# Layer 1 on four split filter steps, tree additions by accumulating transfers, and field copies on GpSimd, in a two-layer interaction kernel

## The reference

```python
z = einsum('bhd,bmd->bhmd', x0, prev)        # products of fields with the layer before
cur = relu(einsum('bpd,pn->bnd', z, W[0]))   # 128 outputs
prev = cur
```

## Time and profile before

| | us |
|---|---|
| median of 3 runs (lowest, highest) | 946.62 (946.28, 947.04) |
| the profiled execution, its own time | 947.22 |
| its span, first to last instruction | 945.3 |
| PE busy | 881.0 |
| DVE busy | 765.0 |
| ACT busy | 691.3 |
| POOL busy | 773.2 |

### The profile page before, as it was taken

How to read it: one execution, slowest core, us unless ns; L and a number is a source line. 1 busy time by engine, 2 the same in 40 slices (tenths; PEclk the granted TensorE clock), 3 DMA queues, 4 the chain that set the end, 5 groups by cost and what they waited for, 6 DMA issues and landing times.

```text
span 945.3 us, 17955 instructions
## 1 busy us (share of the span) xinstructions
PE 881.0 (93%) x3551; PEld 650.2 (69%) x3551; DVE 765.0 (81%) x2391; ACT 691.3 (73%) x2347; POOL 773.2 (82%) x582
## 2 busy tenths in 40 slices
PE   0289999999999999999999999999999999999989
PEld 0157777777777777777777777777777777777753
DVE  4068888889888888898888889988888899888893
ACT  2058777787878777878787778787877777877762
POOL 7768899888888999988889989887777877777772
PEclk9999999999999999999999999999999999999999
DMA  6031222222112222221122222211222222102000
GB/s 175 13 105 51 75 75 75 73 72 71 32 50 70 73 74 73 74 71 34 46 69 74 73 74 74 74 38 37 67 71 71 71 71 71 47 29 66 1 1 0
DMA packets 41436, 58.13 MB, mean 61 GB/s; under 512 B 7265, under 2 KB 16033, under 8 KB 41410
## 3 DMA queue, kind: packets, MB, share of 16 engines
q1 hardware_dynamic: 37314, 55.76, 18.6%
q0 software_dynamic: 4096, 2.11, 1.4%
HBM read 54.79 MB, written 3.05 MB: 61 GB/s over the span
## 4 chain that ended last, share of the span: by engine, by line
PE 53%; DVE 26%; issue 14%; POOL 4%; DVEq 2%; DMA 0%; ACT 0%
PE bank L836 38%; DVE acc L721 18%; PE bank L774 12%; POOL rows L331 4%; DVE pair L587 4%; DVE cur_low L598 2%; DVE parts L721 1%; DVEq L718 1%; PE bank L879 1%; DVEq L240 0%; PE bank L866 0%; PE bank L867 0%; DVE sum L629 0%; PE bank L874 0%; DVEq L707 0%
## 5 line engine op out<-in xcount | busy, mean ns | idle before, releaser
L521 ACT ACTIVATE parts<-bank,x 128x128 f32<-128x128 f32 x2048 | 584.8, 385 | 143.5 <-PE bank L836 140.1
L721 DVE SCALAR_TENSOR_TENSOR acc<-bank,x,acc 128x128 f32<-128x128 f32 x1792 | 485.6, 343 | 97.2 <-PE bank L836 96.0
L836 PE MATMUL bank<-w_high,cur_high 128*128 128x512 f32 x1024 | 440.5, 430 | 10.9 <-DVE acc L721 10.0
L836 PE MATMUL bank<-w_low,cur_high 128*128 128x512 f32 x1024 | 401.4, 392 | 0.0
L836 PE MATMUL bank<-w_high,cur_low 128*128 128x512 f32 x992 | 389.1, 392 | 0.0
L352 POOL TENSOR_TENSOR half<-parts 128x1024 f32<-128x1024 f32 x127 | 307.1, 2418 | 92.4 <-DVE parts L721 91.9
L836 PEld LDWEIGHTS bank<-w_high,cur_high 128*128 128x128 f32 x1024 | 192.5, 188 | 105.9 <-DVE acc L721 29.3
L836 PEld LDWEIGHTS bank<-w_low,cur_high 128*128 128x128 f32 x1024 | 193.0, 188 | 48.8 <-issue 14.8
L836 PEld LDWEIGHTS bank<-w_high,cur_low 128*128 128x128 f32 x992 | 186.4, 188 | 41.8
L352 POOL TENSOR_TENSOR half<-half 128x512 f32<-128x512 f32 x127 | 165.5, 1303 | 10.0
L378 POOL DMA_INDIRECT rows_next<-table_dram,ids_next x96 | 92.5, 963 | 17.5 <-issue 7.0
(11 more groups left out here) (77 smaller groups left out, 485.8 us busy)
## 6 DMA issues: line engine op xcount, KB each, us to landing
shifts<-x_scratch SPq DMA_DIRECT2D x155, 256.0 KB
x<-x_scratch SPq DMA_DIRECT2D x31, 256.0 KB, 2.9
x_scratch<-turned SPq DMA_DIRECT2D x31, 64.0 KB, 1.5
rows_next<-table_dram,ids_next POOLq DMA_INDIRECT x96
wt<-w_top_dram SPq DMA_DIRECT2D x2, 512.0 KB, 8.9
x_scratch<-turned SPq DMA_DIRECT2D x31, 32.0 KB, 1.8
rows<-table_dram,ids_sb POOLq DMA_INDIRECT x32, 2.4
w_sb<-w_ab_dram SPq DMA_DIRECT2D x1, 256.0 KB
```

The costliest lines, as they stand in the source:

```text
L521: ins = nc.scalar.activation(parts[q][ab][:, at:at + N2], act_bank[ab][:, i * N2:(i + 1) * N2], ACT.Copy, scale=x0[u][:, h, 2 * q + ab:2 * ...
L721: nc.vector.scalar_tensor_tensor(out=dst, in0=dve_bank[e % 2 * 2 + ab][:, i * N2:(i + 1) * N2], scalar=x0[u][:, h, 2 * q + ab:2 * q + ab + ...
L836: return nc.tensor.matmul(dst[:], cur_half[u][:, cols], w1_half[:, fields], **flags)
```

## The change

Layer 1's steps 1 to 4 are all split; the slots of the side work are new. The tree's first addition is made by an accumulating transfer that POOL issues for each tile. There is one `left`; POOL adds its halves too (`sum_left`), ACT rectifies the total (slot 20) and DVE adds it (slot 24). The copies for x0 and `turn_in` are POOL's.

```diff
-TREE = 3
-LEFTS = 2
+TREE = 2
+LAST_TREE = 3
-SPLIT = (1, 2)
+SPLIT = (1, 2, 3, 4)
-ACT_PAIR_HIGH = {5: 1, 13: 2}
-ACT_HIGH16, DVE_LOW16 = 9, 12
-PE_PRODUCT = {17: 1, 19: 3, 21: 0, 23: 4, 24: 2}
+ACT_PAIR_HIGH = {5: 1, 8: 2, 9: 3, 16: 4}
+ACT_HIGH16, DVE_LOW16 = 12, 16
+PE_PRODUCT = {18: 1, 19: 2, 21: 3, 22: 0, 24: 4}
-ACT_X0 = 21
-ACT_TURN, PE_TURN, ACT_TURNED = 1, 6, 8
-ACT_LEFT, DVE_TOTAL, DVE_FOLD = 20, 24, 28
+PE_TURN, ACT_TURNED = 3, 4
+ACT_TOTAL, DVE_FOLD = 20, 24
...
+            def add_halves(pair_no, q, whole):
+                pool.wait_ge(act_prod, (pair_no + 1) * (2 * EACH))
+                pool.wait_ge(mac, (pair_no + 1) * (2 * MACS))
+                nc.gpsimd.tensor_tensor(mark[:], mark[:], mark[:], ALU.subtract)
+                width = EACH * HG * N2 // 2
+                for ab in range(2 if whole else 1):
+                    nc.gpsimd.dma_start(parts[q][ab][:, 0:width], parts[q][ab][:, width:2 * width],
+                                        accum_op=ALU.add).then_inc(added[ab], 16)
             def sum_parts(chunk, pair_no, t):
...
+                pool.wait_ge(added[t % 2], (pair_no + 1) * 16)
+                src = parts[t // 2 % 2][t % 2]
+                nc.gpsimd.tensor_tensor(half[t % 2][:], src[:, 0:512], src[:, 512:1024], ALU.add).then_inc(tree, 1)
+                pool.wait_ge(tree, tile * TREE + 1)
+                nc.gpsimd.tensor_tensor(left[:, t % DC, :, :].rearrange("p l n -> p (l n)"),
+                                        half[t % 2][:, 0:256], half[t % 2][:, 256:512], ALU.add).then_inc(tree, 1)
+            def sum_left(chunk):
+                pool.wait_ge(tree, (chunk + 1) * (DC * TREE))
+                pool.wait_ge(total_rectified, chunk + 1)
+                nc.gpsimd.tensor_tensor(total.rearrange("p (t n) -> p t n", t=DC), left[:, :, 0, :], left[:, :, 1, :],
+                                        ALU.add).then_inc(totalled, 1)
...
             def block_body(k, next_block, one_after):
+                for t in range(0, tiles, 2):
+                    whole = next_block or t < tiles - 2
                     if t % DC == 0 and (next_block or t < tiles - DC):
+                        pair_lows(k * CPB + t // DC + 1, (2, 3))
+                    add_halves(k * (tiles // 2) + t // 2, t // 2 % 2, whole)
+                    for s in (t, t + 1):
+                        if (next_block and s < rows_at) or (one_after and s > rows_at):
+                            for f in late[s]:
+                                gather(f)
+                    if t % DC == 0:
+                        if next_block or t < tiles - DC:
+                            copy_x0(k, t // DC + 1)
+                        if next_block or t // DC + 3 < CPB:
+                            copy_turn_in(k, t // DC + 3)
+                    if t % DC == 2 and (next_block or t < tiles - DC - 2):
+                        pair_lows(k * CPB + t // DC + 2, (0, 1))
+                    for s in (t, t + 1) if whole else (t,):
+                        sum_parts(k * CPB + t // DC, k * (tiles // 2) + t // 2, s)
+                        if s % DC == DC - 1:
+                            sum_left(k * CPB + t // DC)
...
-        def act_left(act, c, u, pairs_before):
+        def act_total(act, c, pairs_before):
+            act.wait_ge(totalled, c + 1)
             act.wait_ge(paired, pairs_before)
+            nc.scalar.activation(x4_bank[:], total, ACT.Relu).then_inc(total_rectified, 1)
...
         def dve_fold(dve, c, k):
+            dve.wait_ge(total_rectified, c + 2)
+            nc.vector.tensor_tensor(block_sum(k), x4_bank[:], block_sum(k), ALU.add).then_inc(folded, 1)
...
             if step == order[0]:
-                wait(pe, summed, c)
-                if turn:
-                    pe.wait_ge(turned_ready, c + 1)
-                if pair16_bank(c) is cur_bank:
-                    pe.wait_ge(low16, c + 1)
+                pe.wait_ge(low16, c + 1)
```

More of the change, by code:

```diff
@@ L94, in dlrm_tower @@
         shifts = [sb(f"shifts_{i}", [P, STEPS, COLS]) for i in range(2)]
-        pair = [sb(f"pair_{i}", [P, COLS]) for i in range(STEPS - 1)]
+        pair_low = [sb(f"pair_low_{i}", [P, COLS], FP32R) for i in range(STEPS - 1)]
+        raw = [sb(f"pair_{i}", [P, COLS]) for i in range(4)]
+        pair = [raw[i % 4][:] for i in range(STEPS - 1)]
         pair_high = {step: sb(f"pair_high_{step}", [P, COLS], FP32R) for step in SPLIT}
-        pair_low = {step: sb(f"pair_low_{step}", [P, COLS], FP32R) for step in SPLIT}
         pair16_hl = sb("pair16_hl", [P, COLS], FP32R)
@@ L116, in dlrm_tower @@
         parts = [[sb(f"parts_{i}{j}", [P, EACH * HG * N2]) for j in range(2)] for i in range(2)]
-        half = sb("half", [P, 1024 + 512])
+        half = [sb(f"half_{i}", [P, 512]) for i in range(2)]
+        mark = sb("mark", [P, 1])
         sum2 = sb("sum2", [P, BLOCKS, DC, N2])
@@ L131, in dlrm_tower @@
         z1_half = free[:, (H1 + H2) // P * B:][:, 0:BLOCKS * 2 * P].rearrange("p (k h b) -> p k h b", k=BLOCKS, h=2)
-        lefts = free[:, 0:LEFTS * DC * 2 * N2].rearrange("p (i t l n) -> p i t l n", i=LEFTS, t=DC, l=2)
-        left = [lefts[:, i, :, :, :] for i in range(LEFTS)]
+        left = free[:, 0:DC * 2 * N2].rearrange("p (t l n) -> p t l n", t=DC, l=2)
+        total = free[:, DC * 2 * N2:DC * 3 * N2]
         z2, y_sb = pair[1], pair[0][0:1, 0:B]
@@ L361, in pair_lows @@
                     pool.wait_ge(pair_high_done, (c - 1) * len(SPLIT) + i + 1)
-                    pool.wait_ge(multiplied, products_before(c, step))
-                    nc.gpsimd.tensor_tensor(pair_low[step][:], pair[step - 1][:], pair_high[step][:].bitcast(FP32),
+                    nc.gpsimd.tensor_tensor(pair_low[step - 1][:], pair[step - 1], pair_high[step][:].bitcast(FP32),
                                             ALU.subtract).then_inc(pair_low_done, 1)
@@ L387, in block_body @@
             def block_body(k, next_block, one_after):
-                for t in range(tiles if next_block else tiles - 1):
-                    if t % DC == DC - 1 and (next_block or t < tiles - DC - 1):
-                        pair_lows(k * CPB + t // DC + 2, (0,))
+                for t in range(0, tiles, 2):
+                    whole = next_block or t < tiles - 2
                     if t % DC == 0 and (next_block or t < tiles - DC):
[L393 to L401, removed]
+                        pair_lows(k * CPB + t // DC + 1, (2, 3))
[15 more added lines that the diff above has]
+                            sum_left(k * CPB + t // DC)
+                        if next_block and s == rows_at:
+                            pool.wait_ge(gathered, (k + 1) * (F * 16))
+                            nc.gpsimd.tensor_copy(
+                                rows[:, bass.ds(k + 1, 1), :, :].rearrange("p o f d -> p (o f d)"),
+                                rows_next[:].rearrange("p f d -> p (f d)")).then_inc(rows_ready, 1)
+                            if one_after:
+                                fetch_ids(k + 2)
@@ L402, in block_body @@
                             pool.wait_ge(rows_ready, k + 2)
-                    if (next_block and t < rows_at) or (one_after and t > rows_at):
-                        for f in late[t]:
-                            gather(f)
             pool.wait_ge(first_gathered[0], (F - LAST_TABLES) * 16)
             pool.wait_ge(first_gathered[1], LAST_TABLES * 16)
-            nc.gpsimd.memset(half[:, 0:1], 0.0).then_inc(rows_ready, 1)
+            nc.gpsimd.memset(mark[:], 0.0).then_inc(rows_ready, 1)
@@ L410, in _ @@
+            pool.wait_ge(rows_ready, 1)
             fetch_ids(1)
@@ L449, in act_x4 @@
             nc.scalar.copy(x4_bank[:], x4[u][:]).then_inc(x4_ready, 1)
-        def act_left(act, c, u, pairs_before):
-            act.wait_ge(tree, (c + 1) * (DC * TREE))
+        def act_total(act, c, pairs_before):
+            act.wait_ge(totalled, c + 1)
             act.wait_ge(paired, pairs_before)
-            nc.scalar.copy(x4_bank[:].rearrange("p (t n) -> p t n", t=DC),
-                           left[u][:, :, 0, :]).then_inc(left_copied, 1)
+            nc.scalar.activation(x4_bank[:], total, ACT.Relu).then_inc(total_rectified, 1)
         def act_pair_high(act, c, step):
             act.wait_ge(paired, paired_at(c, step))
-            wait(act, multiplied, products_before(c, step))
-            nc.scalar.copy(pair_high[step][:], pair[step - 1][:]).then_inc(pair_high_done, 1)
+            nc.scalar.copy(pair_high[step][:], pair[step - 1]).then_inc(pair_high_done, 1)
         def act_high16(act, c):
@@ L509, in body @@
                                 slot = q * 2 * GROUPS + 4 * e + ab
[L511 to L514, removed]
                                 if e == 0:
@@ L532, in body @@
                                     act_high(act, c + 1, 1 - u)
[L533 to L537, removed]
+                                if slot == ACT_TOTAL and not (first and u == 0):
+                                    act_total(act, c - 1,
```

(25 more changed lines are left out.)

47 lines of the change are left out of this document (27 added, 20 removed).

## The result

The changed kernel takes 965.07 us, median of 4 runs (964.03 to 966.81), against 946.45 of before: 1.0199 times as long, 95% interval 1.0181 to 1.0217. The profiled execution took 964.03 us, its span is 962.2. The prediction was 961.0, in a range of 950 to 1010.

A forecast was written before the change was run, and what follows sets the result against it. A loop through DVE and PE was taken as the bound: 30 loops by 0.40 = 12.0, + 1.0 - 0.6 + 2.0 = +14.4 us, 961.6 on the profiled execution and 961.0 as median; range 950 to 1010.

The forecast's parts named there:

- What bounds: One chunk's loop: DVE from cur_low to low16 13.17 us, then 0.95, then PE to next cur_low 12.68; sum 26.80.
- `low16` behind the group, the fold out: DVE's part of the loop: +2.07 us for the group of slot 12, -0.60 for the fold moved to slot 24.
- The 0.11 that I was unsure of: Before, low16 started 0.71 us after step 4, not 0.60; if that belonged to the order, the sum is +0.33.
- Products: PE's part behind low16: -0.69 us for the first product one slot later, -0.34 for two more split steps.
- Sum: Whole loop of a chunk: +0.44 us, or +0.33 if 0.11 belonged to the old order; +0.40 taken.
- PE's wait: PE, after slot 18, idles about 1.4 us before the first product, with low16 as releaser.
- POOL covered: POOL needs about 26 us a chunk, with 1 us of transfer waits, just under the loop: no cost, little cover.
- the doubled reading: Accumulating transfers: if reading the destination doubles the moving, landing takes 5.4 us and POOL waits some 2.9 at one pair.
- Rival A: POOL and its transfers become the bound, needing 27.1 to 29.1 us a chunk: 990 us, 967 to 1010; chance 0.36.
- Rival B: DVE's multiply-adds get faster without POOL's four 2.4 us reads of parts: 943 us; chance 0.09.
- The ends: First and last chunks: +1.0 us for chunk 0, -0.6 for the last chunk, +2.0 for POOL's last tile.
- The last tile: Kernel's end: DVE waits for POOL's issue, landing and additions, 7.0 to 8.7 us with the mark: +2.0 in the middle.

The follow-up runs named there:

- e2: Kernel before with only low16 (slot 12 to 16), ACT's rounding for it (9 to 12) and the first product (17 to 18) moved; 1015.57 us.
- e3: Changed kernel with steps 3 and 4 plain again (no rounding by ACT, no rest by POOL for them); 970.60 us, ratio 1.0218.
- e4: Changed kernel with DVE's fold back at slot 28, behind cur_low; 979.92 us, ratio 1.0308.
- e1: Changed kernel with low16 back at slot 12, before that slot's multiply-adds; 923.55 us, ratio 0.9716.
- e8: Changed kernel with PE's layer 1 products after slots 20, 21, 22, 23, 24 instead of 18, 19, 21, 22, 24; low16 unmoved; 922.30 us.
- e6: Changed kernel with one more 512-column POOL addition per chunk in the first three blocks; 965.08 us, ratio 1.0187.
- e7: Changed kernel with three more 512-column POOL additions per chunk in the first three blocks; 1043.54 us, ratio 1.1038.

## Why the prediction was right

The forecast was +14.4 us on the profiled execution; it was +16.8, and +18.6 between the medians. The mechanism was the forecast one, and the periods were 27.25 and 27.54 us for the 27.2 and 27.5 written down. The sum is nearer than its parts: the 30 loops took 14.3 us for 12.0 and chunk 8 another 1.45, and the ends 1.2 for 2.4, so that the misses partly cancel. That is luck.

- **What bounds.** The loop through DVE's stretch and PE's stretch: e2, e3 and e4 each change one part of it, and the period moved by 1.37, 0.25 and 0.52 for the 1.38, 0.34 and 0.60 counted. e1 and e8 take 2.07 and 1.38 out of it, and the period fell by 1.43 and 1.40, to 25.8 in both: there PE's own work takes over.
- **`low16` behind the group, the fold out.** Forecast +2.07 - 0.60 = +1.47; `cur_low` to `low16` went from 13.17 to 14.70, +1.53. The 0.11 that I was unsure of stayed (`low16` follows the group after 2.19, not 2.07), and the fold was worth 0.52 to 0.55 (e4), not 0.60, as the first multiply-add now follows `cur_low` after 0.65.
- **Products.** Forecast -0.69 - 0.34 = -1.03; it is 11.72 - 12.68 = -0.96, and from `low16` to product another -0.12 (0.83 for 0.95). The plain products' 0.35 is e3's.
- **Sum.** +0.46 for the 0.33 to 0.44 counted, of which I took 0.40. The first of the 30 loops took 0.90 more (27.08 for 26.18), since in it, too, no fold had stood before; I had counted that for the loop ahead of it alone.
- **PE's wait.** 1.15 us idle for the 1.4 forecast, `low16` as releaser.
- **POOL covered.** It was, and by less than I wrote: a landing of 5.3 us, not 3.7, and 52 us of waiting for transfers, 1.6 a chunk for the 1.0 taken. The price came almost to that of the doubled reading (85 engine-us a MB is 1.7 times the plain rate), the upper bound; the issue was 1.07 for 0.96, and the two copies, put at 0.3 us each without a row, took 0.56 and 0.52 in the mean. Rival A still did not come: e6 shows 1.3 us free, e7 that 3.9 are not. The Trainium skill, in "Collectives: The Full Stack", section "The bandwidth ceiling: the fold count and why AG ≠ RS ≠ AR", has adding half as fast as copying in a collective's ring. The trace nearly agrees with 1.7; but the two queues also differ in their rows and in where they read, and that the second read is the cause was not tested.
- **Rival B.** A group of 8 takes 2.07 as before (341.61 to 343.68 in the row below): the big reads of POOL had cost the multiply-adds nothing. They did cost DVE's other additions, as the last section shows.

```profile
341.61 2.16 DVE L733 SCALAR_TENSOR_TENSOR acc<-bank,x,acc 128x128 f32<-128x128 f32 x8
343.68 0.69 DVE L605 TENSOR_TENSOR bank<-bank,shifts 128x512 f32<-128x512 f32 x1
```

- **The ends** are the part that failed. I had +1.0, -0.6 and +2.0; it was +1.35 to the second `cur_low` and -0.16 from the last one on. The last chunk's loop took DVE 26.0 us for 29.2, mostly since two additions with both inputs in SBUF took 2.27 and 0.56 instead of 3.37 and 2.61 (before first, then now):

```profile
900.23 3.37 DVE L696 TENSOR_TENSOR w_sb<-sum 128x1024 f32<-128x1024 f32 x1
909.24 2.61 DVE L616 TENSOR_TENSOR rows_next<-w_sb 128x384 f32<-128x384 f32 x1
...
917.29 2.27 DVE L708 TENSOR_TENSOR w_sb<-sum 128x1024 f32<-128x1024 f32 x1
925.20 0.56 DVE L634 TENSOR_TENSOR rows_next<-w_sb 128x384 f32<-128x384 f32 x1
```

  The last tile cost +1.9 (forecast +2.0), and the stretch after it 1.1 more, with the clock at 0.94 from 945 to 962 us (1.00 before). At the start `cur_low` of chunk 0 came 3.8 us later, with the clock at 0.86 from 50 to 60 us (1.00 before). All of that went into DVE's wait for `shifts`, which fell from 4.4 to 0.6: the step behind it starts at 61.98 for 62.07. From there to the second `cur_low` it is 24.67 us for 23.23, +1.44 for the +1.0 counted.
- **Not foreseen:** chunk 8, 1.45 us, for which the last section has the rows.

## What to carry to other kernels

Find the loop that passes through the engines, write its terms down in order, and ask of each operation which part it stands in: here one DVE operation was worth 0.5 us a chunk or nothing, and one slot number 41 us (965 to 924). When something is moved past a group of work, count the whole group. When a cover is tested with extra work, look first for the earliest deadline, not for the engine's idle time.

## What the runs showed of the hardware that I had not expected

**The clock falls after short waits of PE.** Idle times of 1.15 us once a chunk left it at 1.00 (2.4 GHz) in the stretches I read; with 1.84 us (e2) it fell, in half of the chunks, in the one shown to a mean of 0.58 over 3 us, toward the lower level of 1.2 GHz. What decides between the halves I did not find.

**POOL idles where its loop turns back**, 2.5 to 3.4 us in seven of the twelve profiles, after the first block, with nothing to wait for that the profile shows. In the changed kernel it is:

```profile
297.31 2.51 POOL L371 TENSOR_TENSOR pair_low<-pair,pair_high 128x512 fp32r<-128x512 f32 x2 [3.04 <-issue]
```

and PE then waits for that `pair_low`:

```profile
298.63 0.50 PE L783 MATMUL bank<-pair_high,w_high 128*128 128x512 f32 x1 [1.17 <-POOL pair_low L371]
```

In e1 the wait is 3.02 us and the clock falls after it (0.50 from 286.5 to 291.5): 5.9 us for one turn of a loop. Three runs bear on the cause. With one more addition before the turn (e6) the idle time is 1.14 us, with three (e7) there is none; so what POOL waits for runs beside its last operations. In e3, where POOL has no `pair_low` to make there, it waits for DVE at that place (3.14 us), and chunk 8 is as long as its neighbours. The queue of kind instruction moves 20 packets in the whole run of the changed kernel, and one of them in this idle stretch (294.5 to 297; packets, MB, share of the 16 engines):

```profile
q14 instruction: 1, 0.01, 0.8%
```

In all seven profiles such a packet lies in the idle stretch, and POOL goes on some 1 to 2 us after it; in e6 and e7 it lies beside the added operations. That POOL waits for its code to be loaded is thus likely; no run was made to test it.

**Additions on DVE beside POOL's.** The last tile's tree took DVE 3.97 and 1.37 us before, beside POOL's additions, and 1.95 and 0.42 now, beside POOL's mark, issue and wait for its transfer. Before, then now:

```profile
921.41 3.97 DVE L738 TENSOR_TENSOR parts<-parts 128x1024 f32<-128x1024 f32 x2
925.42 1.37 DVE L738 TENSOR_TENSOR w_sb<-parts 128x256 f32<-128x256 f32 x1
...
935.23 1.95 DVE L750 TENSOR_TENSOR parts<-parts 128x1024 f32<-128x1024 f32 x2
937.22 0.42 DVE L750 TENSOR_TENSOR w_sb<-parts 128x256 f32<-128x256 f32 x1
```

POOL in the same stretch, where the mark takes 1.24 us for the 0.19 of others, so POOL is held up too:

```profile
935.27 1.24 POOL L342 TENSOR_TENSOR mark<-mark 128x1 f32<-128x1 f32 x1 [0.85 <-DVE parts L733]
936.46 0.88 POOL L345 DMA_DIRECT2D parts<-parts  x1
941.08 1.25 POOL L353 TENSOR_TENSOR half<-parts 128x512 f32<-128x512 f32 x1 [3.74 <-DMA parts<-parts]
```

The multiply-adds, with one input in PSUM, show none of it (2.07 us a group, above). This is the lock that the Trainium skill describes in "SBUF — State Buffer", section "Who interferes with whom", and the trace agrees with these numbers.
